# Scaled angles in a recurrent scan, one reduction in place of two sums, and moved work at three borders, on one core

## The reference, cut to what matters

```
layer 0: attention over x (one head tiled 16 times), then a routed 8-expert FFN with a shared FFN
layer 1: a GRU over the 256 positions, then a low-rank expert layer with a base matrix
layer 2: an RK4 scan over the 512 columns' states, driven by x, then retrieval of 64 experts out of 4096
layer 3: attention with 8 heads, then low-rank experts
```

```
i_couple = jnp.tanh(q) @ coupling.T
dq = q - q ** 3 / 3.0 - p + drive + i_couple + bias
dp = EPSILON * (q + ALPHA - BETA * p)
...
q_next = q + DT / 6.0 * (dq1 + 2 * dq2 + 2 * dq3 + dq4)
p_next = p + DT / 6.0 * (dp1 + 2 * dp2 + 2 * dp3 + dp4)
q_next = jnp.clip(q_next, -CLAMP, CLAMP)
```

## Time and profile before

| | |
|---|---|
| median of 3 runs | 5117.64 us (5112.13 to 5129.14) |
| the profiled execution | 5103.12 us, span of its instructions 5101.5 us |
| busy PE, weight load, DVE, ACT, POOL | 4800.1, 3821.7, 2819.2, 1521.0, 298.2 us |
| attn0 and moe0 | 0 to 749 us |
| gates | to 923 us |
| GRU steps alone (32) | 923 to 1064 us |
| joint steps with GRU (224), without (32) | 1064 to 2712, 2712 to 2944 us |
| retrieve_experts | 2945 to 4365 us |
| attn3, lora3 | to 5101 us |

### The profile page before, as it was taken

How to read it: one execution, slowest core, us unless ns; L and a number is a source line. 1 busy time by engine, 2 the same in 40 slices (tenths; PEclk the granted TensorE clock), 3 DMA queues, 4 the chain that set the end, 5 groups by cost and what they waited for, 6 DMA issues and landing times. The chain is left out here.

```text
span 5101.5 us, 196672 instructions
## 1 busy us (share of the span) xinstructions
PE 4800.1 (94%) x83696; PEld 3821.7 (75%) x83696; DVE 2819.2 (55%) x16412; ACT 1521.0 (30%) x6006; POOL 298.2 (6%) x867
## 2 busy tenths in 40 slices
PE   8899989799999999999997599999989999999999
PEld 3335654599999999999996587889979999444434
DVE  4110011479999999999998735675553432344421
ACT  1100111234444444444443322233322222233330
POOL 1010010001111111111111100000000000000000
PEclk7899999655555555555555599999989999999999
DMA  2202430000000000000001000034320000100000
GB/s 83 102 35 80 169 125 17 15 4 5 5 5 5 5 5 5 5 5 5 5 5 53 3 20 1 2 86 99 93 85 3 3 3 3 45 9 8 8 8 33
DMA packets 52290, 159.57 MB, mean 31 GB/s; under 512 B 13873, under 2 KB 14001, under 8 KB 46272
## 3 DMA queue, kind: packets, MB, share of 16 engines
q1 hardware_dynamic: 45408, 130.70, 7.8%
q0 software_dynamic: 3712, 12.29, 0.7%
q10 hardware_dynamic: 2304, 4.20, 0.2%
HBM read 129.63 MB, written 17.17 MB: 29 GB/s over the span
## 5 line engine op out<-in xcount | busy, mean ns | idle before, releaser
L621 PE MATMUL k_ps<-k_hl,k_wlo 128*128 128x8 f16 x16384 | 607.2, 169 | 141.1 <-ACT k_hl L697 136.7
L621 PEld LDWEIGHTS k_ps<-k_hl,k_wlo 128*128 128x128 f16 x16384 | 533.6, 105 | 177.3 <-ACT k_hl L697 160.3
L625 PE MATMUL k_ps<-k_hl,k_whi 128*128 128x16 f16 x16384 | 588.7, 174 | 0.0
L625 PEld LDWEIGHTS k_ps<-k_hl,k_whi 128*128 128x128 f16 x16384 | 516.1, 104 | 0.5
L621 PE MATMUL g_ps<-g_hl,g_wlo 128*128 128x8 f16 x12288 | 436.8, 168 | 41.3 <-DVE g_hl L775 37.2
L625 PE MATMUL g_ps<-g_hl,g_whi 128*128 128x16 f16 x12288 | 441.5, 174 | 0.0
L621 PEld LDWEIGHTS g_ps<-g_hl,g_wlo 128*128 128x128 f16 x12288 | 387.1, 104 | 47.5 <-DVE g_hl L775 42.6
L697 ACT ACTIVATE k_hl<-k_q 128x32 f16<-128x32 f32 x768 | 175.9, 229 | 742.5 <-DVE k_q L732 742.5
L625 PEld LDWEIGHTS g_ps<-g_hl,g_whi 128*128 128x128 f16 x12288 | 387.1, 104 | 0.0
L1446 DVE TENSOR_REDUCE t_NM<-t_ps 128x1 f32<-128x512 f32 x256 | 165.0, 686 | 211.9 <-PE t_ps L1312 211.9
L1218 DVE TENSOR_TENSOR HQ<-p_ior,p_pm 128x2048 f32<-128x2048 f32 x64 | 146.3, 2290 | 223.9 <-PE p_sim L1042 223.9
(11 more groups left out here) (328 smaller groups left out, 8902.0 us busy)
## 6 DMA issues: line engine op xcount, KB each, us to landing
GRZ<-expert_places SPq DMA_DIRECT2D x64, 512.0 KB, 4.9
wm<-in_w_dram SPq DMA_DIRECT2D x4, 2816.0 KB, 10.4
GRZ<-in_w_dram SPq DMA_DIRECT2D x4, 2816.0 KB, 10.3
m_w<-in_w2a_dram SPq DMA_DIRECT2D x8, 1280.0 KB, 12.6
GRZ<-in_ue_dram SPq DMA_DIRECT2D x8, 1024.0 KB, 7.6
GRZ<-in_x_nat_dram SPq DMA_DIRECT2D x4, 1024.0 KB, 10.5
XT<-in_xT_dram SPq DMA_DIRECT2D x1, 4096.0 KB, 27.0
expert_rows<-wm SPq DMA_DIRECT2D x1, 4096.0 KB, 24.1
```

The source lines that it names most:

```text
L621: T.matmul(P[:,j,1,:],lo[:,kc,(m0+j)*128:(m0+j+1)*128],x[:,kc,0,:],start=(j==0 and kc==0),stop=False,skip_group_check=True)
L625: i=T.matmul(P[:,j,:,:],hi[:,kc,(m0+j)*128:(m0+j+1)*128],x[:,kc,:,:],start=False,stop=kc==KC-1,skip_group_check=True)
```

## The change

Scan: the weights of `coupling` are split with the factor `SK` = DT/2 x 8192, and the state `q` is kept multiplied by `Z` = 8192 x 1024 (by Z/2 for evaluation 3's argument), so that the products come out in the state's own units. ACT's tanh and square take the factor back through their scale. `kl` gets a third part: part 0 is the float16 tanh, part 1 is S times part 0 (`tensor_scalar`, L844), part 2 is S times the float32 tanh minus part 1 (`scalar_tensor_tensor`, L846); the high weights meet parts 1 and 2. `total` writes its sum for k = 0 to 2 into PSUM (`sums`), next to the products but in the other bank, and `end` is one `tensor_reduce` over three terms (L857) for k = 0 to 2; for k = 3 the two instructions remain. POOL's copy becomes a multiplication by 1/Z. `LEAD` goes from 32 to 29, and the four additions of the experts' result all fall on i = 12, two and two.

attn0 and moe0: the last pair's context product is issued ahead of `outputs(NP-2)`, ACT evacuates it ahead of its copies, DVE's reciprocal for it stands between the copies of the pair before, and the load of `sw13` is issued in attn0. Router logits come in two groups of two 8-row blocks (rows 0 and 64), and are turned with 8 matmuls of 16 columns.

retrieve_experts: the first `weights_hot` and `pairs_hot` move into the first loop (tiles 12, 13 and 15), with buffers `B0` of their own; `scatter(0,q)` and ACT's `spread(0,q)` follow the picks of tile 15; `combine(0,0)` no longer stands behind `scatter(1,0)`.

```
-DT=0.01; S=1024.0; SW=64.0; US=1.0/(S*SW)
+DT=0.01; S=1024.0; SW=64.0; US=1.0/(S*SW); SK=DT/2*8192.0; Z=8192.0*S
...
+                if n==2:
+                    e.wait_ge(s_vt,NP)
+                    e.dma_start(side[:,0:8*H].rearrange('p (d n) -> p d n',d=4),sw13_d).then_inc(s_sw,16)
...
-                if n>=1: outputs(n-1)
+                if 1<=n<NP-1: outputs(n-1)
             context(NP-1,3)
+            outputs(NP-2)
             outputs(NP-1)
...
+                if n==NP-1: evac_c(n)
...
-                    for step in range(4): copy_out(e,cp,n-1,1,step)
-            recip(NP-1)
+                    for step in range(4):
+                        copy_out(e,cp,n-1,1,step)
+                        if n==NP-1 and step==1: recip(n)
...
-            for k in range(4):
-                if k>=1: e.wait_ge(s_lc,k)
+            for g in range(2):
                 for d in range(4):
-                    i=T.matmul(ps[6][0:8,:],wg[:,d,:],C0T[:,d,k*512:(k+1)*512],start=d==0,stop=d==3)
+                    for x in range(2):
+                        i=T.matmul(ps[6-2*g][x*64:x*64+8,:],wg[:,d,:],C0T[:,d,(2*g+x)*512:(2*g+x+1)*512],start=d==0,stop=d==3)
...
-LEAD, TL = 32, 16
+LEAD, TL = 29, 16
...
-        psk=[c.enter_context(nc.psum_tensor(f'k_ps{i}',[128,512],F32)) for i in range(2)]
+        psk=c.enter_context(nc.psum_tensor('k_ps',[128,1024],F32))
+        terms=[psk[:,o:o+672].rearrange('p (s x) -> p s x',s=3)[:,:,0:32] for o in (100,300)]
+        products=[terms[0][:,0:2],terms[1][:,1:3]]; sums=[terms[0][:,2],terms[1][:,0]]
...
-                group(psk[k%2],clo,chi,kl,0,k_lo,t*4+k+1,k_mm)
+                for j in range(KC):
+                    for kc in range(KC):
+                        T.matmul(P[:,1,j*NB:(j+1)*NB],clo[:,kc,j*128:(j+1)*128],kl[:,kc,0,:],start=(j==0 and kc==0),stop=False,skip_group_check=True)
+                e.wait_ge(k_lo,2*(t*4+k+1))
+                for j in range(KC):
+                    for kc in range(KC):
+                        i=T.matmul(P[:,:,j*NB:(j+1)*NB],chi[:,kc,j*128:(j+1)*128],kl[:,kc,1:3,:],start=False,stop=kc==KC-1,skip_group_check=True)
+                i.then_inc(k_mm,1)
...
-                    A.activation(kl[:,:,0,:],m4(src),ACT.Tanh).then_inc(k_hi,1)
-                    A.activation(Tt[:],src,ACT.Tanh).then_inc(k_t,1)
+                    unit=2/Z if k==3 else 1/Z
+                    A.activation(kl[:,:,0,:],m4(src),ACT.Tanh,scale=unit).then_inc(k_hi,1)
+                    A.activation(Tt[:],src,ACT.Tanh,scale=unit).then_inc(k_t,1)
...
-                    G.tensor_copy(HQ[:,:,:,t-1],m4(q[:,0,:])).then_inc(k_out,1)
+                    G.tensor_scalar(HQ[:,:,:,t-1],m4(q[:,0,:]),1/Z,None,ALU.mult).then_inc(k_out,1)
...
-                elif i in (12,13):
-                    dc=2*(i-12)+part
-                    e.wait_ge(l_o,j+1)
+                elif i==12:
+                  e.wait_ge(l_o,j+1)
+                  for dc in (2*part,2*part+1):
...
-                e.wait_ge(k_t,t*4+k+1)
-                V.tensor_tensor_reduce(kl[:,:,1,:],m4(Tt[:]),kl[:,:,0,:],S,0.0,ALU.subtract,ALU.max,lz[:,0:1]).then_inc(k_lo,1)
+                e.wait_ge(k_hi,t*4+k+1)
+                V.tensor_scalar(kl[:,:,1,:],kl[:,:,0,:],S,None,ALU.mult).then_inc(k_lo,1)
+                e.wait_ge(k_t,t*4+k+1); e.wait_ge(k_lo,2*(t*4+k)+1)
+                V.scalar_tensor_tensor(kl[:,:,2,:],m4(Tt[:]),S,kl[:,:,1,:],ALU.mult,ALU.subtract).then_inc(k_lo,1)
...
-                at['S']=ch.did(stt(Sk[:],g[:],-cs[k]/3,base))
+                at['S']=ch.did(stt(Sk[:] if k==3 else sums[k%2],g[:],(-cs[0]/3,-cs[1]/3,-cs[2]/6,-cs[3]*2/3)[k],base))
             def end(t,k):
-                P=view(psk[k%2])
                 e.wait_ge(k_mm,t*4+k+1)
                 ch.after(at['S'])
-                n_v=ch.did(stt(m4(v[:]),P[:,1],cs[k]*US,m4(Sk[:])))
-                ch.after(n_v)
-                stt(m4(qn[:] if k==3 else q[:,k+1,:]),P[:,0],cs[k]/SW,m4(v[:])).then_inc(k_q,1)
+                if k<3: V.tensor_reduce(q[:,k+1,:],terms[k%2].rearrange('p s x -> p x s'),AX.X,ALU.add).then_inc(k_q,1)
+                else:
+                    n_v=ch.did(stt(v[:],products[1][:,1],1/3,Sk[:]))
+                    ch.after(n_v)
+                    stt(qn[:],products[1][:,0],1/3,v[:]).then_inc(k_q,1)
...
+                    if i==NTL-1: scatter(0,q)
...
-            for q in range(4): scatter(0,q)
             for i in range(NTL):
                 for q in range(4):
-                    scatter(i+1,q)
+                    if i>=1: scatter(i+1,q)
+                    elif q==3: scatter(1,2); scatter(1,3)
                     combine(i,q)
+                    if i==0 and q<2: scatter(1,q)
...
+                    if i==NTL-1 and q<3: pairs_hot(q+1)
...
-            for q in range(4): pairs_hot(q)
-            weights_hot(0)
-            for q in range(3): pairs_hot(4+q)
+                if i==NTL-4: weights_hot(0)
+                if i==NTL-3: pairs_hot(0)
+            for q in range(1,4): pairs_hot(4+q)
+            pairs_hot(4)
             weights_hot(1)
-            pairs_hot(7)
```

85 lines of the change are left out of this document (47 added, 38 removed).

## The result

| | before | after |
|---|---|---|
| median of 18 runs | 5120.93 us (5105.44 to 5137.49) | 5100.04 us (5083.31 to 5116.27) |
| ratio | | 0.996, 95% interval 0.9949 to 0.9971 |
| the profiled execution | 5103.12 us | 5111.15 us |

The account below looks back on a forecast made before the run. It took the chain from state to state, not PE's fullness, to bound the scan's steps. Scan -34, attn0 to moe0 -10 and retrieve_experts -24 made -67 from a median of 5117.6: 5051 us, range 5016 to 5088.

Parts of the forecast that it names:

- The reduction: Scan: one reduction replaces `v` and `q`, taking 0.26 us; product to tanh 0.29 instead of 0.45 us.
- Both rivals on a dearer reduction: Scan: reduction of 0.32 us, +31, 5082 us (chance 0.12); or paying by output, 67 us gone at 0.38 us (0.04).
- The rest of the operand: Scan: L846 starts about 0.21 us after L844, high matmuls at +0.76 instead of +0.73.
- The hold by POOL: Scan, evaluation 0: POOL's copy holds L844 to +0.53, so L846 starts 0.08 us later; bounds 0 and 0.18.
- No hold: Rival, scan: L844 runs free of POOL, 0.08 us a step over 256 steps, -20: 5031 us; chance 0.20.
- PE's pace, DVE's list: Joint scan steps: PE sets evaluation 2 at 1.72 us; DVE's list holds evaluation 3's `v`, tanh at 1.93.
- LEAD and the additions: Scan: three GRU steps alone go, -12.8 us; the experts' additions cost 1.1 a block instead of 0.6, +6 us.
- attn0 and moe0: attn0 to moe0: last outputs 5.8 us sooner, router 3.8 us shorter; together -10 us.
- retrieve_experts: retrieve_experts: matrices and scatters moved into tile 15's picks shorten PE's wait, -23.7 us.
- The bound of -15: retrieve_experts: the smaller gain, -15 us, if the waits leave PE at its lower clock; other bound -27.
- The forecast's own case: Whole kernel: the forecast's terms hold, 5051 us, own range 5036 to 5068; chance 0.51.
- borders: Rival, attn0 to moe0 and retrieve_experts: nothing gained, PE waits for the next thing instead, +34, 5085 us; chance 0.07.

Follow-up runs that it names:

- experiment 7: The changed kernel without its reduction: two instructions sum in every evaluation, the sum in SBUF; 5216.02 us, +116 against after.
- experiment 4: The changed kernel with L846's two waits exchanged, first for L844, then for the second tanh; 5047.79 us, ratio 0.9857, -52 against after.
- 8: The changed kernel with the product made by ACT and the rest by DVE's one custom instruction of before; 4999.67 us, ratio 0.9768, -100 against after.
- 9: The changed kernel without the factor 1024 in the coupling: L844 gone, L846 one subtraction; 4995.58 us, ratio 0.9763, -104 against after.
- Experiment 11: The changed kernel without the factor 1024 in the coupling, and with tile 0's four scatters behind tile 15's picks as before; 4991.44 us, ratio 0.9752.
- experiment 3: The changed kernel with L844 written as a scalar_tensor_tensor instead of a tensor_scalar; 5120.5 us, ratio 1.0003, +20 against after.
- 5: The changed kernel in which L844 waits for both tanh and L846 for L844 alone; 5187.34 us in one run, +87 against after.
- experiment 2: The kernel before with the change's borders, LEAD 29 and the four additions in one step, evaluations as before; 5078.96 us, ratio 0.9924.

## Why the prediction was wrong, step by step

**The reduction: right.** 0.254 was read off the line of the earlier trace rows; measured over all 768 (line in a window: ns min/median/max):

```profile
L857 DVE TENSOR_REDUCE k_q<-k_ps x768: 249/258/259, 1049.5 to 2950.8; 128x32 f32<-128x96 f32 x192
```

The page's group of it has the mean:

```profile
L857 DVE TENSOR_REDUCE k_q<-k_ps 128x32 f32<-128x96 f32 x768 | 196.4, 256 | 32.8 <-PE k_ps L650 9.2
```

Against the line from contiguous groups three addresses far apart cost nothing. Both rivals on a dearer reduction fall; experiment 7 gives its worth.

**The rest of the operand: the step that failed.** "L846 starts about 0.21 after L844" took the 0.03 between dependent DVE instructions from pairs that have one wait, or the late wait first. L846's code waits for the tanh and then for L844, which comes later. The trace of before has such pairs only where something else holds the start too (L739, with its late wait second, starts 0.12 after L779's end in the joint steps, in a full list of DVE; in the steps of the GRU alone it waits for ACT), so the 0.03 had no bound above it, though the text asked for one from both sides. Measured 0.28; its price is 52 us (experiment 4). The high matmuls of evaluation 1 then come at +0.84, those of evaluation 0 at +0.79, and `v` of evaluation 3 at +1.55 instead of +1.48. The Trainium skill (Perfetto Trace Analysis, Identifying Dependency Chains) says that instructions that wait for several engines may get EventSemaphore instructions in front with the further conditions. The traces agree: it is the wait written second that gets one, and a late one costs 0.104 us from the producer's end instead of 0.034 (experiment 4). The page says nothing of order or cost. Why the extra instruction costs 0.07 us is not shown; that it stands between the two is.

**The hold by POOL: absent.** In the trace of after L844 takes this long:

```profile
L844 DVE TENSOR_SCALAR k_hl<-k_hl x1024: 164/172/243, 1048.3 to 2951.4; 128x32 f16<-128x32 f16 x171
```

In evaluation 0 it starts at +0.26, 0.01 before POOL's multiplication, and takes 0.17 though POOL works beside it for 0.34. In 20 evaluations POOL had begun first (5 of them evaluation 0, 15 evaluation 3); in 19 of those L844 took 0.17 as well, in one 0.243. So the row of attn0 (2.33 us) doesn't carry over to an instruction of 32 numbers in half precision. Whether size, type or POOL's instruction makes the difference was not tested. The hold would have put L846 at +0.56, the late wait put it at +0.54, so evaluation 0 came out as forecast (1.86 against 1.87) by luck, for a wrong reason. With the waits in order it is 1.78, the 0.08 of the rival "No hold".

**The two errors together.** With the waits in order the scan takes 1845.8 us, 35 less than before, where the forecast had 21 less; the whole kernel has 5048 us, next to the forecast 5051. As made, the scan loses 25.

**The rest of the experts' work: not in the sum.** Over a block of 16 steps the joint steps exceed their median by 0.9 us before and by 2.3 after, also with the waits in order (2.2). The additions explain half of the growth (0.6 a block more); the other 0.7 a block, some 10 us in all, are in other steps of the block. No experiment took this apart. So the closeness of 5048 and 5051 is partly luck: the missing hold (-20 by the rival) outweighs this.

**PE's pace, DVE's list: right.** Evaluation 2 runs at 1.71 in after and in experiments 4, 8, 9 and 11 (1.72 forecast), bound by four groups of 16 matmuls at a granted clock of 0.50, and evaluation 3 is the longest, since DVE's list holds `v`. Where the operand comes later still, evaluation 2 is longer (1.73 in experiment 3, 1.84 in 5). The page of after shows both new places in one line each (columns as in a group of the page; the last part is the idle time ahead and its releaser):

```profile
L650 PE MATMUL k_ps<-k_hl,k_whi 128*128 128x16 f16 x16384 | 606.7, 175 | 12.5 <-DVE k_hl L846 11.3
...
L846 DVE SCALAR_TENSOR_TENSOR k_hl<-k_T,k_hl 128x32 f16<-128x32 f32 x1024 | 197.2, 193 | 111.0 <-DVE k_hl L844 5.5
```

DVE's 111 us idle ahead of L846 is 0.108 a time. With the waits in order it is 39.1 us, 0.038 a time.

**LEAD and the additions: right.** -12.8 alone; 1.0 (experiment 2) to 1.2 (after) a block against 1.1.

**attn0 and moe0: mechanism right, one half missed.** The rows that answer:

```profile
157.21 3.94 PE L159 MATMUL a_ps<-a_wos,a_CT 16*128 16x256 f32 x16 [4.10 <-POOL a_CT L236]
...
168.00 9.07 PE L372 MATMUL m_ps<-HQ,m_wg 128*8 128x512 f32 x32 [3.43 <-DMA m_wg<-in_wg_dram]
178.37 1.96 PE L377 MATMUL m_ps<-ident,m_lg 72*128 72x16 f32 x16 [1.30 <-ACT m_lg L445]
180.18 15.27 PE L387 MATMUL m_ps<-HQ,GRZ 128*128 128x512 f32 x35
```

The outputs come 7.6 us sooner against the same pair's context (5.8 forecast). The forecast held the reciprocal behind two copies; in after it starts 2.6 us after the end of ACT's copy `a_CS`, when the DMA behind that lands, as before, and the copies hold nothing. From logits to shared FFN it is 12.2 us; before it was 24.3 (to 183.72 in the trace of before). The forecast had -3.8 of these -12.1 (its terms add up to -3.7): the waits and the small products. It overlooked the logits themselves: 32 records took 17.0 us before (6.24 for the first group, mostly at the low clock, then three times 3.60) and take 9.07 now. At the full clock one record started every 0.43 us before; now two start 0.003 us apart every 0.43 (at the low clock one every 0.85 before, two every 0.85 now). The two groups of eight outputs, written to partitions 0 and 64, run at the same time. That the array's tiles can work at the same time is what the Trainium skill (TensorEngine Tiling (Array Packing), Key Properties) says; this trace agrees, and the forecast should have weighed it. The rest, 2.3, is the FFN's start: between 184 and 190 us the granted clock is 0.61 before and 1.00 after.

**retrieve_experts: the wait was moved, at the low clock.** The bound of -15 "if the waits leave PE at its lower clock" was the right case, and even that was not reached (-10). The picks of tile 15 in after (ns min/median/max, first and last start; then what ended PE's idle time: us, times):

```profile
L1054 PE MATMUL p_sim<-GRZ,HQ x256: 222/268/313, 3736.6 to 3760.5; 128*64 128x32 f32 x128
...
  issue: 5.5, 2
  ACT GRZ L1125: 2.5, 2
```

The windows (columns as above):

```profile
3735.00:3745.00 10.00, 6.47 (x258) 6.08 (x257) 7.89 (x6) 3.10 (x4) 0.00 (x0) 1.00 0.86 336
3745.00:3755.00 10.00, 8.91 (x249) 8.62 (x250) 4.20 (x4) 1.92 (x2) 0.00 (x0) 0.54 0.22 88
3755.00:3765.00 10.00, 9.34 (x276) 9.07 (x272) 5.69 (x5) 2.52 (x3) 0.00 (x0) 0.50 0.34 109
```

PE stands 2.7 us at 3742.6, in the middle of a pick, in a stretch in which the DMA engines are full (0.86 and 336 GB/s over the window); in the next window its clock is 0.54, then 0.50. Picks and scatters then take 3.63 us instead of 2.06, and the last product comes 14 to 15 us later than before (by the two profiles of before) instead of 4.7, a figure for which the forecast gives no working. That is 9 to 10 of the 14 us missed. The rest stands behind `scatter(1,0)`: PE waits 1.5 us for nothing that the profile shows in a scatter at 3800.6, and the `combine` behind it, at the low clock in part, takes 9.6 us instead of 7.4. Experiment 11 shows that the product's lateness isn't what decides, either: with it gone, the waits shown there take its place.

**The chances.** The forecast's own case held 0.51 and its rivals were about other steps (hold, reduction, borders). None was "one of the two dependent steps starts later", though each 0.01 us of it costs about 256 x 3 x 0.01 = 8 us. That was the place for a rival.

## What to carry to other kernels

Where a DVE instruction waits for two things, write the wait for the one that comes last first; in a loop of 1024 dependent rounds this one exchange was 1% of the time, and no count of instructions shows it. (Whether the order matters on other engines was not tested.) When a change puts a second dependent instruction into a chain, bound its start from both sides by pairs with the same waits, and ask whether another engine, or other units, can take the first one out of the chain: here that was worth another 48 us. And look at matmuls with few output columns as candidates for pairs in different column groups before counting their waits.
